# Experts stage: residual, norm and write-back of rows moved ahead of the linear stage

## The reference

```
x = layernorm(x + dilated_attention(x))
x = layernorm(x + moe(x))           # router: softmax over 8 experts, the best one only
x = layernorm(x + linear_attention(x, W))
x = layernorm(x + soft_moe(x, phi, W, b))

moe(x):  e = argmax(x @ router_w + router_b);  a, g = split(x @ w1[e]);
         y = (silu(a) * g) @ w2[e];  return y * max_prob
linear_attention:  q, k, v = split(x @ W);  q, k = elu(q) + 1, elu(k) + 1
         KV = k^T v;  out = q KV / (q . sum(k) + eps)
```

## Time and profile before

| | us |
|---|---|
| median of 3 runs | 1465.41 (1462.29 to 1465.42) |
| the profiled execution, its own time | 1451.5 |
| its span, first to last instruction | 1449.5 |
| TensorE busy in the span | 1364.7 (94%) |
| VectorE, ScalarE, GpSimd busy | 916.3, 656.9, 737.9 |
| routing, from its tables to the end | about 156 to 180 |
| experts | 182.4 to 553.8 |
| linear attention, first transpose | 575.5 |

### The profile page before, as it was taken

How to read it: one execution, slowest core, us unless ns; L and a number is a source line. 1 busy time by engine, 2 the same in 40 slices (tenths; PEclk the granted TensorE clock), 3 DMA queues, 4 the chain that set the end, 5 groups by cost and what they waited for, 6 DMA issues and landing times. The chain is left out here.

```text
span 1449.5 us, 28607 instructions
## 1 busy us (share of the span) xinstructions
PE 1364.7 (94%) x9049; PEld 1192.0 (82%) x9050; DVE 916.3 (63%) x1927; ACT 656.9 (45%) x1206; POOL 737.9 (51%) x677
## 2 busy tenths in 40 slices
PE   8997799999999993999989999999999989999997
PEld 4554688888888882777779999999999979999997
DVE  5888453333333334677588798888888854566656
ACT  4554333333333332666554453453443435555553
POOL 6663178655640004231059887887887957140300
PEclk9998799999999996999999999999999999999999
DMA  4112343342200004120043365465465486465450
GB/s 171 51 40 74 135 150 98 135 154 98 101 15 14 14 15 145 59 59 1 1 131 95 103 181 156 135 187 144 138 184 139 143 270 241 156 217 189 161 201 29
DMA packets 112539, 171.43 MB, mean 118 GB/s; under 512 B 6400, under 2 KB 97664, under 8 KB 106336
## 3 DMA queue, kind: packets, MB, share of 16 engines
q1 hardware_dynamic: 103456, 156.27, 33.4%
q0 software_dynamic: 3408, 9.31, 2.3%
q10 hardware_dynamic: 5616, 5.11, 1.0%
HBM read 115.22 MB, written 55.44 MB: 118 GB/s over the span
## 5 line engine op out<-in xcount | busy, mean ns | idle before, releaser
L2134 PE MATMUL comb_psO<-hand_parts,comb_eh 128*128 (+1 forms) x1024 | 198.2, 291 | 0.5 <-DVE hand_parts L1548 0.5
L1799 ACT ACTIVATE disp_raw<-disp_psL 128x512 f32<-128x512 f32 x128 | 76.6, 598 | 197.8 <-PE disp_psL L1711 112.3
L2134 PEld LDWEIGHTS comb_psO<-hand_parts,comb_eh 128*128 128x128 f32 x1024 | 157.1, 190 | 0.8 <-issue 0.7
L1105 DVE TENSOR_TENSOR moe_hs<-moe_psH,moe_act_a 128x512 f32<-128x512 f32 x78 | 50.2, 686 | 159.0 <-PE moe_psH L999 149.7
L1711 PE MATMUL disp_psL<-disp_ph,hand_xh 128*128 (+1 forms) x512 | 147.6, 288 | 0.8 <-DVE disp_e L1984 0.8
L2253 DVE TENSOR_TENSOR comb_el<-comb_psT,comb_eh 128x512 fp32r<-128x512 f32 x128 | 88.0, 688 | 91.0 <-ACT comb_eh L2168 88.7
L1711 PE MATMUL disp_psL<-disp_ph,hand_xl 128*128 (+1 forms) x512 | 144.9, 283 | 0.0
L1711 PE MATMUL disp_psL<-disp_pl,hand_xh 128*128 (+1 forms) x512 | 144.7, 283 | 0.0
L2134 PE MATMUL comb_psO<-hand_parts,comb_el 128*128 (+1 forms) x512 | 144.3, 282 | 0.0
L1735 PE MATMUL disp_psS<-disp_e,last_x 128*128 128x256 f32 x512 | 133.5, 384 | 4.1 <-POOL disp_e L1893 4.1
L1210 POOL DMA_INDIRECT lin_yg<-sorted_y,table_place x32 | 32.4, 1011 | 190.7 <-POOLq L905 143.2
(11 more groups left out here) (294 smaller groups left out, 3740.2 us busy)
## 6 DMA issues: line engine op xcount, KB each, us to landing
logits<-disp_raw SPq DMA_DIRECT2D x64, 512.0 KB, 4.0
hand_e<-logits SPq DMA_DIRECT2D x32, 1024.0 KB, 6.3
w_raw<-in_w SPq DMA_DIRECT2D x8, 2048.0 KB, 7.9
disp_wt<-in_w_slot SPq DMA_DIRECT2D x16, 1024.0 KB, 10.0
w_raw<-in_w SPq DMA_DIRECT2D x8, 1024.0 KB, 10.6
slot_y<-disp_slots SPq DMA_DIRECT2D x64, 128.0 KB, 3.2
disp_bt<-in_b_slot SPq DMA_DIRECT2D x15, 512.0 KB, 5.2
comb_y_in<-slot_y SPq DMA_DIRECT2D x3, 2048.0 KB, 10.5
```

The costliest lines, as they stand in the source:

```text
L1105: v.tensor_tensor(hs[:, cols], psH[:, 2 + h, :], act_a[:, cols], ALU.mult).then_inc(hs_ready, 1)
L1799: nc.scalar.activation(raw[mc % 4][:, half * 2:half * 2 + 2, :], psL[l_bank[mc]][:, half * 2:half * 2 + 2, :], ACT.Copy).then_inc(copied, 1)
L2134: last = nc.tensor.matmul(psO[j % 2][:, 0:D], ep[s % EB][:, i, :], yp[:, bass.ds(odd, 1), ch * D:(ch + 1) * D].rearrange("p a d -> p (a d) ...
```

## The change

- Routing: the product that gives `token` has a third group of 40 columns, that counts the rows in each place (1 or 0). From it DVE makes `dest`, the row that a place goes back to; an unused place gets a spare row of its own behind the 4096. A second row of 32 products (`psP`, 120 columns) takes the probabilities, cut in three bf16 parts, to slot order (`share`). The first gather waits for the count 8 in place of 5 of the same semaphore, and `keep_turning` has 12 transposes in place of 38.
- Experts: all gathered rows stay in one tile `every`. DVE adds both halves of `psY`, times `share`, to the slot's rows (two operations), takes the moments, and every four slots does the chain for mean and root, in two parts (`root_start` in the third step of four, `root_end` in the fourth). The chain's scratch tiles lie in unused columns of `psX`'s bank, so that an operation reads at most one tensor from SBUF. ACT norms a slot eight steps after it was loaded. The last three slots have chains of their own: slots 36 and 37 together, then 38.
- POOL, after the last weights are split, puts the normed rows back in `x2_dram` by `dest`, a slot a transfer. Slots 0 to 30 wait until the transfer of the slot before has landed; the last eight wait only for the one four slots before.
- SP loads the linear stage's weights during the experts, and when all rows are back the first 8 tiles in four pieces of two.
- Linear attention: no gathers, no residual, no norm at the start; the projections' input is loaded as it is.

```diff
@@ normalise_and_route
             pool.wait_ge(stored, 16 * B)
-            pool.wait_ge(tables_ready, 5)
+            pool.wait_ge(tables_ready, 8)
...
             last.then_inc(counted, 1)
-            keep_turning(nc, c, psX[1][:, 0, 0, :], 38)
+            pe.wait_ge(tables_ready, 7)
+            for t in range(NT):
+                last = nc.tensor.matmul(psP, rows1[:, t // TG, :, t % TG], shares[:, t // TG, :, t % TG], start=t == 0, stop=t == NT - 1)
+            last.then_inc(counted, 1)
+            keep_turning(nc, c, psX[1][:, 0, 0, :], 12)
...
+            link(v.reciprocal(route["prob"][:], tmp[:]))
+            link(v.tensor_copy(part[0][:], route["prob"][:]))
+            link(v.tensor_tensor(left[:], route["prob"][:], part[0][:], ALU.subtract))
+            link(v.tensor_copy(part[1][:], left[:]))
+            link(v.tensor_tensor(part[2][:], left[:], part[1][:], ALU.subtract))
...
+            for a in range(3):
+                v.tensor_tensor(shares[:, :, a * NCOL:(a + 1) * NCOL, :], slots1, over_r(part[a][:], NCOL), ALU.mult).then_inc(tables_ready, 1)
@@ class Gathers
+    def put_back(self, pool, slot, out_dram):
+
+        q = slot % 4
+        if 0 < slot < SLOTS - 8:
+            pool.wait_ge(self.landed[(slot - 1) % 4], 16 * (self.issued((slot - 1) % 4) + (slot - 1) // 4 + 1))
+        pool.wait_ge(self.landed[q], 16 * (self.issued(q) + slot // 4))
+        self.nc.gpsimd.indirect_dma_start(out_dram, bass.IndirectOffsetOnAxis(self.route["dest"][:, slot:slot + 1], 0),
+                                          self.kept(slot), None).then_inc(self.landed[q], 16)
@@ experts, sync
+            early.load_weights(sp)
+            gathers.wait_put_back(sp)
+            for i in range(early.PIECES):
+                early.load_piece(sp, i)
@@ experts, gpsimd
+            for t in range(SLOTS):
+                pool.wait_ge(normed, t + 1)
+                gathers.put_back(pool, t, x2_dram)
+            gathers.wait_put_back(pool)
@@ experts, tensor
                     wait(pe, xl_ready, t)
+                    wait(pe, stat, t - 2)
@@ experts, scalar
-                    nc.scalar.activation(yo[q % 2][:], psY[:, 0:D], ACT.Copy).then_inc(yo_ready, 1)
...
+                t = s - 8
+                if live(t):
+                    norm(t, q, i - 1)
@@ experts, vector
-                    v.tensor_tensor(yo[q % 2][:], psY[:, D:2 * D], yo[q % 2][:], ALU.add).then_inc(yo_ready, 1)
+                    v.scalar_tensor_tensor(gathers.kept(t), psY[:, 0:D], share, gathers.rows(t), ALU.mult, ALU.add).then_inc(added, 1)
+                    dve.wait_ge(added, 2 * t + 1)
+                    v.scalar_tensor_tensor(gathers.kept(t), psY[:, D:2 * D], share, gathers.kept(t), ALU.mult, ALU.add).then_inc(added, 1)
...
+                if q == 2 and not (isinstance(i, int) and i == 0):
+                    dve.wait_ge(stat, i * 4)
+                    root_start(i - 1, 0, 4, 0)
+                if q == 3 and not (isinstance(i, int) and i == 0):
+                    root_end(i - 1, 0, 4, 0, i * 4 - 4)
+                if isinstance(s, int) and s == SLOTS + 1:
+                    dve.wait_ge(stat, SLOTS - 1)
+                    root_start(WHOLE, 0, REST - 1, 4)
+                    root_end(WHOLE, 0, REST - 1, 4, 0)
+                t = s - 2
+                if live(t):
...
+                    v.bn_stats(stats[:, (q + 2) % 4, :], gathers.kept(t)).then_inc(stat, 1)
+                if isinstance(s, int) and s == SLOTS + 1:
+                    dve.wait_ge(stat, SLOTS)
+                    root_start(WHOLE + 1, REST - 1, 1, 4 + REST - 1)
+                    root_end(WHOLE + 1, REST - 1, 1, 4 + REST - 1, 0)
@@ linear_attention
-            for t in range(2 * TB):
-                fetch(t)
...
-                    if s < B and j < TB // 2:
-                        residual(s, 2 * j)
-                        residual(s, 2 * j + 1)
-                    if s < B and j == TB // 2:
-                        root_in(s)
```

More of the change, by code:

```diff
@@ L953, in experts, with quads @@
         halves = [slice(h * (FK // 2), (h + 1) * (FK // 2)) for h in range(2)]
-        ys_tiles = ys_dram.rearrange("(t p) d -> t p d", p=P)
+        ROOT_START = 12
+        ROOT_LINKS = ROOT_START + 4 * NEWTONS
+        WHOLE = SLOTS // 4
+        REST = SLOTS - 4 * WHOLE
+        def quads(eng, step):
+            for t in range(8):
+                step(t // 4, t % 4)
+            with eng.Fori(2, WHOLE) as i:
+                for q in range(4):
+                    step(i, q)
+            for t in range(4 * WHOLE, SLOTS + 2):
+                step(t // 4, t % 4)
         def live(t):
@@ new lines, in root_end @@
+            def root_end(n, first, count, place, used):
+                link = linking(n * ROOT_LINKS + ROOT_START)
+                dve.wait_ge(chain, n * ROOT_LINKS + ROOT_START)
+                at = slice(place, place + count)
+                me, va, ro, tm, ro2 = (tile[:, at] for tile in (mean, var, guess, tmp, guess2))
+                for a in range(NEWTONS):
+                    last = a == NEWTONS - 1
+                    link(v.tensor_tensor(tm, ro, ro2, ALU.mult))
+                    link(v.scalar_tensor_tensor(tm, tm, -0.5, va, ALU.mult, ALU.mult))
+                    if last:
+                        wait(dve, normed, used)
+                    link(v.scalar_tensor_tensor(ro2, tm, 1.5, ro, ALU.add, ALU.mult),
+                         v.scalar_tensor_tensor(rstd[:, at] if last else ro, tm, 1.5, ro, ALU.add, ALU.mult))
+                v.scalar_tensor_tensor(drop[:, at], me, -1.0, ro2, ALU.mult, ALU.mult).then_inc(rooted, 1)
@@ L1098, in step @@
+            def step(i, q):
+                s = i * 4 + q
                 t = s - 1
@@ L1364, in _ @@
                         finish(s - 1, 2 * (j - 2) + 1)
-                    if s + 1 < B and j >= 6:
-                        for a in range(3):
-                            norm_in(s + 1, 3 * (j - 6) + a)
                 wait(act, added, s * TB + TB)
```

259 lines of the change are left out of this document (140 added, 119 removed).

## The result

The kernel after takes 1472.84 us (median of 6 executions, 1468.87 to 1478.45), the kernel before 1463.62 beside it (6 executions): a ratio of 1.0075, with an interval of 1.0057 to 1.0093. It is slower by 0.75%, or 11 us (the medians lie 9.2 apart); 1460.7 was forecast, and 1457.0 to 1467.5 as the range.

A forecast was written before the change was run, and what follows sets the result against it. TensorE was taken to bound the experts, the gap behind them being what the change could reach. Handover -5.3, routing +0.3, experts +0.3 and linear stage 0 gave -4.7: 1465.4 became 1460.7 us, range 1457 to 1467.5.

The forecast's parts named there:

- The two adds, chains, moments, norm, put-back: Handover from the last `psY`: DVE, ACT and POOL work on the last slots, last put-back landed at 567.6.
- The rival of dearer small operations: DVE's chains and `root_end`: steps on PSUM cost more, at 0.40 us each 8 us slower, 1473; chance 10%.
- step 6: Handover: POOL's last put-back lands 2.9 us after issue, at 567.6; the skill's rule on HBM writes would make it more.
- all engines leave the experts when POOL has seen the last landing, 567.6 and some 0.5: End of the experts: the stage's end adds only some 0.5 us after the last put-back lands.
- they have 2.6 us of cover: Handover: the weights' split on ACT and DVE ends near 571.5, hidden before the projection at 574.1.
- step 7: Handover: SP loads four pieces of 256 KB; first there at 569.6, last by 573.2, taken as 573.1.
- Transfers before the last: Experts, POOL: put-backs of slots 0 to 30 start at 414.4, take 3.0 us each, catch up and cost nothing.
- If the weights' load sets that pace, 120 columns cost no more: Routing, TensorE: 32 products stay at 5.0 us; routing +0.3, or 2 to 3 later if columns set the pace.
- So 0.8 us are left and TensorE waits for nothing: Experts, every fourth slot: `root_end` and moments take 3.1 of 3.9 us; experts +0.3, between -0.3 and 2.7.
- Linear stage: After the handover: removing residuals and norms, which lie under TensorE's projections, changes 0, at best 1 us less.
- The base: Whole kernel: the runs' median lies 13.9 us above the profiled execution's 1451.5, so 1465.4 is the starting time.
- The fourth: Routing 2 to 3 us later or chains 1.6 us more, making the gain -3 to 0, 1464; chance 20%.

The follow-up runs named there:

- e12: The kernel after, unchanged, run again on another chip where the kernel before takes 1462 us: ratio 1.0073 to the kernel before.
- e16: The kernel before, unchanged, profiled on a chip where it takes 1462 us: ratio 1.0009.
- e6: The kernel after with the experts' block ended without GpSimd's drain: ratio 1.0042 to the kernel before, handover 20.2 us.
- e11: e10 plus identity transposes on TensorE, 24 and 64 in the routing and 12 at the linear stage's start: ratio 0.9979 to the kernel before.
- e14: e10 plus 12 identity transposes on TensorE at the linear stage's start: ratio 0.9976 to the kernel before.
- e13: The kernel before, unchanged, profiled on a chip where it takes 1450 us: ratio 0.9999.
- e10: The kernel after with no drain, pieces issued in the linear stage, 80 columns, scaled mean from PSUM, register loads before TensorE's wait: ratio 0.9964 to the kernel before.

## Why the prediction was wrong, by its own steps

What the change costs on one kind of chip comes from e12 against e16: routing +5.9 us from first `psI` to first `psX`, experts +7.5, handover -1.0, rest +1.2, and -0.6 ahead of `psI`: 12.9 us of span, but for rounding. The ratio 1.0073 makes it 10.7. The forecast had +0.3, +0.3, -5.3 and 0, in all -4.7. Of the 17.6 us between the two, routing is 5.6, the experts 7.2, the handover 4.3 and the rest 1.2. So three steps failed. Routing and experts each cost more than the 4.7 us that were forecast to be gained, so either turns the sign by itself. The stage's end doesn't: without the drain e6 is still 0.42% slower than before.

- **The two adds, chains, moments, norm, put-back**: right. The adds took 0.96 together (1.04 forecast), each chain 3.7 us (4.3): a step with operands in PSUM takes 0.20, like one in SBUF. Norm 0.60, the last put-back landed after 2.5 (2.9). The rival of dearer small operations is out. So is, for this transfer, what step 6 quotes from the Trainium skill (DMA: Bandwidth & Descriptors, Anatomy of one DMA) on writes to HBM: in e6 the 39 put-backs, which write it, landed sooner than the gathers (median us, last figure).

```profile
x_rows<-moe_xg,table_dest POOLq DMA_INDIRECT x39, 2.4
moe_xg<-x_rows,table_token POOLq DMA_INDIRECT x38, 2.8
```

- **"all engines leave the experts when POOL has seen the last landing, 567.6 and some 0.5"**: wrong. It is 6.8 us, by POOL's drain of 6.36, 4.4 of which the handover gets back without it. A hint was within reach: the earlier trace rows name `POOLq L905` as what ended 143 us of POOL's idle time, the block's end, and the drain of 7.85 stands at that line. Before the change the put-backs weren't there, so POOL was drained long before it mattered.
- **"they have 2.6 us of cover"**, of the weights' split: it went with the step above; the split started at 599.5 and made TensorE wait 1.95 us. What would be late next was named rightly. A small slip beside it: step 7's own figures, 567.6 and 5.8, make 573.4 and not 573.2.
- **Transfers before the last**: their pace was 3.1 us (3.0 forecast), their start 439.6 instead of 414.4, and it made no difference: they caught up by 521.
- **"If the weights' load sets that pace, 120 columns cost no more"**: wrong, and chosen against the right alternative ("0.235 each", "token 2.5 later": 0.226 and 1.9 later). That alternative was then undersized, "the whole stage 2 to 3": if 120 columns take 7.2 us, the second 32 products do as well, and they took the place of transposes that cost less: 2.2 + 7.2 + 2.7 - 6.5 is 5.6. The clock that was to rise behind them rose later, as the transposes were fewer, but e11 shows for 80 columns that it would not have mattered to these products.
- **"So 0.8 us are left and TensorE waits for nothing"**: right for the array and wrong for its sequencer, which needs 1.8 us behind the wait before it can issue the next product. It costs 0.5 eight times, 4.0 us in all, and idle time of TensorE every fourth slot is one of the prediction's own signs of being wrong. The locked operation was not thought of at all; slot 7 takes 4.9 us more in e12 than in e16. Against these stands a gain beyond the lower bound of -0.3: without both losses the experts take 371.8 us (e14), 2.2 less than e13's 374.0 on the same chip, as every second slot of before takes 9.5 us and those of e14 9.4.
- **Linear stage**: +1.2 in e12 against e16 instead of 0, and +0.7 to +3.4 over the nine profiles of after and its single edits, against the kernel before on the same kind of chip. Of the 1.2 and of after's, 0.6 to 0.7 lie in the first 96 products for `psK` (57.2 against 56.5 us in e12); the rest stays open. Where the five edits are together it is gone (870.2 in e10).
- **The base**: 13.9 us were added for the difference of the profile to the runs. It is about what lies between the two kinds of chip, and it did no harm, since it cancels.

None of the four rivals was it. The fourth had the right place for one term, the routing, and too small a price, 2 to 3 us for 5.6.

## What to carry to other kernels

When an engine's last work moves to the end of a stage, count what the stage's end itself does on that engine: POOL's drain took 6.4 us behind 77 indirect transfers here and 3.1 to 3.2 behind 32 and 38, free for as long as POOL is done early. A wait that is over before the array needs it can still be late for the sequencer: add up what stands behind it, loads of registers above all. And compare profiles only from chips on which the same kernel takes the same time; a profile of the kernel before on such a chip showed that nearly half of the difference was none of the change's.

## What the hardware showed beyond that

Products whose columns lie 16 bytes apart took 5.0 us for 32 of 80 columns at either clock, and 1.7 ns for each further column. A drain that is left out is paid by POOL at its next one. Small DVE operations that read and write PSUM cost no more than those in SBUF (0.20 a step), and one that scales 4 values in SBUF took 4.03 us beside POOL's. An indirect transfer to HBM of 128 rows landed in 2.4 us in the median of e6, sooner than a gather from it (2.8). On three chips ACT stopped for 8 to 15 us while POOL's gathers ran, and with it DVE, in all eleven profiles taken there and for both kernels; on two others, in none of seven.
